# Image quarters on 128 partitions, folded normalisation, norms from the squared image and patches by chunk, in a patch-attention kernel

## The chip, the core and the metric

One NeuronCore of a Trainium2 chip. The time is that of one execution on the device, in microseconds (us). A core has TensorE (matmul, PE, with its weight loads PEld), VectorE (DVE), ScalarE (ACT), GpSimd (POOL), and SyncE (SP), which here issues DMAs.

## What is computed

The input x is 2 images of 32 channels, 48x48. Cut to what matters:

```python
x1 = x + L0(gn(x))            # gn: every channel of every image to mean 0, variance 1
out = x1 + dct2(gn(x1))       # cosine transform over rows and columns

# L0, per image:
embed = prelu(Wa x + ba)                            # 32 channels, 48x48
match = prelu(W1 x + b1)                            # 16 channels, 48x48
ref   = prelu(W2 mean2x2(x) + b2)                   # 16 channels, 24x24
w     = patches(ref, 3)                             # 576 keys of 144
w     = w / max(norm(w), 1e-4)
y     = softmax(10 * w @ patches(match, 3), axis=keys)     # 576 keys x 2304 queries
yt    = transposed_conv(y, patches(embed, 6, stride 2), stride 2)
return (conv(yt, Wd, 3x3, stride 2) + bd) / 6
```

All products are made nearly in fp32, from a high part (fp32r) and the low rest of each operand.

## The kernel before

**Queries.** The 2304 queries of an image are 6 groups of 384 (`CHUNK`): group t holds image rows t, t+6, t+12, ... Each group is 3 tiles of 128 queries, so there are 12 groups and 36 tiles for both images.

**Start (list `BEFORE`, image 0).** SyncE loads x three times, on partitions 0 to 95 (`load_x`), in a part of 768 columns and one of 1536. VectorE takes statistics (L893), GpSimd the power -1/2 (L444), VectorE normalises in two halves (L910), ScalarE rounds to fp32r (L733), VectorE makes the low part of the third copy (L918). A convolution is then one matmul per piece with high and low weights stacked over the 96 rows (L542 with four strided reads for the 2x2 mean, L549). ScalarE makes the negative and the positive part of each piece (L749, L751) and VectorE joins them with the slope into the padded images `wimg` and `mimg` (L942). SyncE's `im2col` copies 144 shifted rows to `wim`/`wim8` (keys) and `vim`/`v2` (queries), six transfers for each image, whole images at a time. The squares of the patches (L790, L791) give the norms by 12 fp32 matmuls (L579, L583), GpSimd the power -1/2 (L459), six matmuls spread it (L592), VectorE scales the keys (L995, L997) and the keys are split in high and low (L797, L798, L1004 to L1006). The embedding (L558, then L971, turned by L569 and split by L769 and L981) is made here too for image 0. The queries of groups 0 and 1 are split by ScalarE (L783, L785) and GpSimd (L468, L472); the first scores (L609) follow.

**Loop.** Step s makes on each engine, in a fixed order: scores of tile s+1 (TensorE, L609), their maximum (VectorE, L1010), the exponential with its sum (ScalarE, L807), its inverse (VectorE, L1017) and the normalisation (ScalarE, L815). GpSimd adds score tiles that meet in an output row (`row_sums`, L478). From step 9 on, three groups behind (`LAG`), the sums of group k are turned (`turn`, L629, five blocks), rounded and split (L823, L1025), multiplied with the embedding (`values`, L644), then with the 3x3 weights (`taps`, L656) and added into x1 (L1048). For t below 9 the scores use two buffers, later one.

**Between.** `SPREAD` puts the preparation of image 1 and the tail of image 0 at gaps: an entry (name, image, n, first, pace) puts part k at gap first + k*pace, that is at step (gap div 3), place (gap mod 3). Each engine performs its share at that place of its own stream, so that what stands behind waits too. `split` of group g stands at gap 9g-10. The buffer `pm` has two places that all small jobs take in turn (`misc`): part n waits until part n-2 has been emptied; `EMPTIES` says by which engine.

**SyncE's queue** is one stream in program order: for each image x, (image 0: parameters), x1's copy of x, (image 0: cosines, the nine blocks of output weights, L374), the patches of `wimg` (L359, L363), those of `mimg`. GpSimd splits the output weights (`output_weights`, L450, L451) between its parts of the start.

## Time and profile before

| | us |
|---|---|
| median of 3 runs (286.1 to 287.36) | 286.29 |
| the profiled execution | 286.1 |
| its span | 284.3 |
| TensorE busy | 216.6 (76%) |
| TensorE weight loads | 200.9 (71%) |
| VectorE busy | 154.6 (54%) |
| ScalarE busy | 137.5 (48%) |
| GpSimd busy | 94.5 (33%) |

The span reaches from the first to the last instruction; the rest of the 1.8 us lies around it. The profile's rows name the line, the engine, the operation, out<-in with the names of the tiles, their sizes and how often (x12). In a time line the first number is the start, the second the time that the group takes; what stands in brackets is how long the engine was idle before it and which work ended that. An fp32 matmul shows as two rows of the trace. "issue" means that nothing shown ended the wait. Granted clock 1.00 is the upper of TensorE's two levels where the throttle is concerned; how fast matmuls follow each other is read from their starts.

### The profile page before, as it was taken

What the parts mean: (1) busy time and instruction counts of PE and PEld (TensorE: products, weight loads), DVE (VectorE), ACT (ScalarE), POOL (GpSimd) and SP (SyncE); (2) the same over time, 40 slices, a digit from 0 to 9 for tenths busy, and PEclk for the clock granted to TensorE, in tenths of its full rate; (3) what the DMA queues carried; (4) which work ended last, traced back from release to release, by engine and by line L of the source; (5) the groups of instructions that cost most, each with busy time, mean ns of one, the idle gap of its engine ahead of it and who ended that gap; (6) DMA issues with size and microseconds to landing.
All of it is one profiled execution on the core that took longest, in us unless ns stands there. A gap on an engine that the chain in (4) does not pass through costs nothing.

```text
span 284.3 us, 4211 instructions
## 1 busy us (share of the span) xinstructions
PE 216.6 (76%) x1522; PEld 200.9 (71%) x1522; DVE 154.6 (54%) x303; ACT 137.5 (48%) x273; POOL 94.5 (33%) x96
## 2 busy tenths in 40 slices
PE   0064755653647998699998999999898999995085
...
## 3 DMA queue, kind: packets, MB, share of 16 engines
...
## 4 chain that ended last, share of the span: by engine, by line
PE 48%; DVE 20%; ACT 12%; issue 9%; SPq 5%; DMA 3%; POOL 2%; DVEq 0%; ACTq 0%; POOLq 0%
PE zt L629 22%; PE yt L644 8%; PE ps L609 6%; DVE negm L1010 4%; DVE bnst L893 4%; PE pm L676 3%; DVE yl L1025 3%; ACT nt L807 2%; SPq L363 2%; ACT zneg L749 2%; PE pd L656 2%; ACT z L751 2%; DVE v L1048 2%; DMA v<-mimg 2%; SPq L359 2%
## 5 line engine op out<-in xcount | busy, mean ns | idle before, releaser
L629 PE MATMUL zt<-ident,nt 128*125 128x128 f32 (+1 forms) x720 | 90.6, 277 | 0.0
L629 PEld LDWEIGHTS zt<-ident,nt 128*125 128x125 f32 (+1 forms) x720 | 87.4, 179 | 0.8
L478 POOL TENSOR_TENSOR nt<-nt 128x599 f32<-128x599 f32 (+1 forms) x42 | 56.9, 1354 | 32.2 <-ACT nt L815 25.0
L1025 DVE TENSOR_TENSOR yl<-zt,yh 125x384 fp32r<-125x384 f32 (+1 forms) x60 | 33.4, 557 | 46.2 <-ACT yh L823 18.2
L823 ACT ACTIVATE yh<-zt 125x384 fp32r<-125x384 f32 (+1 forms) x60 | 29.2, 486 | 36.9 <-PE zt L629 36.9
L807 ACT ACTIVATE nt<-ps,negm 128x576 f32<-128x576 f32 x32 | 23.8, 742 | 44.6 <-DVE negm L1010 44.6
L468 POOL TENSOR_TENSOR ml<-vim,mh 128x384 fp32r<-128x384 f32 x12 | 12.3, 1029 | 61.9 <-ACT mh L783 61.8
L815 ACT ACTIVATE nt<-nt,rps 128x599 f32<-128x599 f32 x36 | 28.7, 797 | 5.0 <-DVE rps L1017 4.8
L1048 DVE SCALAR_TENSOR_TENSOR v<-pd,v 32x384 f32<-32x384 f32 (+3 forms) x48 | 26.3, 547 | 2.6 <-PE pd L656 0.9
L1010 DVE TENSOR_REDUCE negm<-ps 128x1 f32<-128x576 f32 x32 | 24.1, 753 | 4.9 <-PE ps L609 4.7
L644 PE MATMUL yt<-yh,kh 125*128 125x384 f32 (+1 forms) x60 | 24.4, 407 | 2.5 <-DVE yl L1025 2.4
L609 PE MATMUL ps<-wh,mh 128*128 128x288 f32 x64 | 17.4, 357 | 11.6 <-ACT nt L807 6.2
L444 POOL TENSOR_TENSOR mv<-mv,mhalf 96x1 f32<-96x1 f32 (+1 forms) x4 | 2.2, 551 | 59.4 <-DVE mv L898 59.3
L609 PEld LDWEIGHTS ps<-wh,mh 128*128 128x128 f32 x64 | 11.4, 214 | 13.9 <-POOL mr L472 8.2
L644 PE MATMUL yt<-yh,kl 125*128 125x384 f32 (+1 forms) x60 | 20.4, 340 | 0.0
L644 PE MATMUL yt<-yl,kh 125*128 125x384 f32 (+1 forms) x60 | 20.4, 339 | 0.0
L542 PE MATMUL pm<-x,wst 96*96 96x288 f32 x16 | 5.2, 464 | 19.5 <-DVE x L918 19.5
L542 PEld LDWEIGHTS pm<-x,wst 96*96 96x96 f32 x16 | 3.6, 258 | 20.6 <-issue 15.5
L1017 DVE RECIPROCAL rps<-psm 128x1 f32<-128x1 f32 x36 | 5.9, 164 | 21.6 <-ACT nt L807 21.4
L609 PE MATMUL ps<-wl,mh 128*128 128x288 f32 x64 | 15.0, 320 | 0.0
L609 PE MATMUL ps<-wh,ml 128*128 128x288 f32 x64 | 14.7, 314 | 0.0
L609 PE MATMUL ps<-wr,mr 128*128 128x288 f32 x64 | 14.6, 313 | 0.0
...
## 6 DMA issues: line engine op xcount, KB each, us to landing
...
```

The lines of the kernel that those rows point to most:

```text
L468: link(pool.tensor_tensor(by_column_group(ml[:, k, :]), in_column_groups(vim[:, :], i), F(by_column_group(mh[:, k, :])), ALU.subtract))
L478: pool.tensor_tensor(nt[:, dst, (to + 1) * KP + 1:(to + 1) * KP + 1 + n], nt[:, one, (row1 + 1) * KP + 1:(row1 + 1) * KP + 1 + n], nt[:, o ...
L609: last = nc.tensor.matmul(scores_of(t)[:, i, 0:HALF], m[:, k, cols], w[b][:, HALF * i:HALF * (i + 1)], start=n == 0, stop=n == 3)
L629: last = nc.tensor.matmul(turned(zt[:, m % 2, :], n, dh, col, JW), keys_at(tile, r + dr, n, shift), ident[:, :], start=at == 0, stop=at == ...
L644: last = nc.tensor.matmul(yt[:, 0:CHUNK], e[b][0:n, blk, :], y[0:n, blk, :], start=blk == 0 and at == 0, stop=blk == KB - 1 and at == 2)
L807: nc.scalar.activation(strided(nt[:, tile_of(g, jb), :], KP + 1, (KP * HL // 2, 2), (KP, HL // 2), (1, WL)), strided(scores_of(t)[:, 0, :] ...
L815: nc.scalar.activation(tile, tile, ACT.Copy, scale=rps[:, k:k + 1]).then_inc(s_pn, 1)
L823: nc.scalar.activation(yh[0:n, blk, :].rearrange("p (h j) -> p h j", j=W), turned(zt[:, m % 2, :], n), ACT.Copy).then_inc(s_yh, 1)
L893: link(nc.vector.bn_stats(stats[rows, i, :], src[:, CHUNK * i:CHUNK * (i + 1)]))
L1010: nc.vector.tensor_reduce(negm[:, t % 2:t % 2 + 1], scores_of(t)[:, :, 0:HALF], AX.XY, ALU.max, negate=True).then_inc(s_mx, 1)
L1025: nc.vector.tensor_tensor(yl[0:n, blk, :].rearrange("p (h j) -> p h j", j=W), turned(zt[:, m % 2, :], n), F(yh[0:n, blk, :]).rearrange("p ...
L1048: nc.vector.scalar_tensor_tensor(out=image, in0=tap, scalar=1.0 / 6.0, in1=image, op0=ALU.mult, op1=ALU.add).then_inc(s_fin, 1)
```

## The change

- x comes in quarters: 576 columns of each channel on partitions 32q to 32q+31 (`x4`), for both images with buffers of their own. Statistics per quarter (2 x 288 columns) are averaged over the quarters by one matmul (`mean`), and the mean is subtracted and the scale applied not to x but to the weights (`weights`: nine operations on VectorE per image) and to the biases (`bias`: six fp32 matmuls and three operations). GpSimd adds 2x2 pixels (`pooled`).
- A convolution of a piece is three matmuls over 32 rows (high x high, high x low, low x high); conv2 and the embedding go in two quarters each, the embedding with 24 matmuls of 144 columns for each of two parts. The match convolution has eight pieces of 288 columns in place of six of 384.
- In every second piece VectorE makes the negative part itself; VectorE's last operation frees `pm`. 
- `mimg` holds the rows in the order of the groups, with a copied block before and behind, so a row of 48 is written once or twice more in 14 places. The match patches are copied by group: 36 transfers of 384 columns for each image, and `split` of a group waits for its own six.
- The norms come from the squared reference image: squares of three 32-row bands (two on ScalarE, one on GpSimd), 18 fp32 matmuls.
- Image 0's embedding moves into steps 1 to 4; the work of image 1 stands later. The parameters are loaded from ScalarE's queue; the output weights, the cosines and x1's copy come behind the match patches on SyncE's.

Cut to its core:

```diff
@@ tables
-EMPTIES = {"conv2": "act", "conv1": "act", "emb": "act", "ek": "dve", "norm": "dve", "inorm": "dve", "zn": "act", "d1": "dve",
+EMPTIES = {"mean": "dve", "bias": "dve", "conv2": "dve", "conv1": "dve", "emb": "dve", "ek": "dve", "norm": "dve", "inorm": "dve", "zn": "act", "d1": "dve",
 BEFORE = [
-    ("rows", (0, 1, 2)), ("scale", (0, 1)), ("low", (0, 1)), ("conv2", (0, 1)), ("conv1", (0, 1, 2, 3, 4, 5)),
-    ("squares", (0,)), ("norm", (0,)), ("inorm", (0, 1)), ("emb", (0, 1)), ("ek", (0, 1)), ("keys", (0,)), ("split", (0, 1))]
+    ("xs", (0,)), ("mean", (0,)), ("low", (0,)), ("weights", (0,)), ("bias", (0,)), ("conv2", (0, 1)),
+    ("conv1", (0, 1)), ("squares", (0,)), ("conv1", (2, 3, 4)), ("norm", (0,)), ("conv1", (5, 6, 7)),
+    ("inorm", (0, 1)), ("keys", (0,)), ("split", (0, 1))]
 SPREAD = [
-    ("residual", 0, 1, 4, 1), ("rows", 1, 3, 7, 1.5), ("scale", 1, 2, 12, 1), ("low", 1, 2, 13, 1),
-    ("conv2", 1, 2, 16, 1), ("conv1", 1, NCH, 19, 1), ("squares", 1, 1, 28, 1), ("norm", 1, 1, 30, 1),
-    ("inorm", 1, 2, 33, 1), ("keys", 1, 1, 37, 1), ("emb", 1, 2, 39, 1), ("ek", 1, 2, 41, 2), ("residual", 1, 1, 60, 1),
+    ("emb", 0, 2, 4, 2), ("ek", 0, 2, 9, 2), ("xs", 1, 1, 13, 1), ("mean", 1, 1, 15, 1), ("low", 1, 1, 17, 1),
+    ("weights", 1, 1, 20, 1), ("bias", 1, 1, 23, 1), ("residual", 0, 1, 28, 1), ("conv2", 1, 2, 26, 1),
+    ("conv1", 1, 8, 29, 1), ("squares", 1, 1, 33, 1), ("norm", 1, 1, 35, 1), ("inorm", 1, 2, 38, 1),
+    ("keys", 1, 1, 41, 1), ("emb", 1, 2, 46, 2), ("ek", 1, 2, 51, 2), ("residual", 1, 1, 60, 1),
@@ sync
+            def match_patches(b):
+                sp.wait_ge(s_const, 6)
+                sp.wait_ge(s_mimg[b], 1)
+                for t in range(NCH):
+                    if b:
+                        sp.wait_ge(s_split, NCH * (b - 1) + t + 1)
+                    im2col(mimg, 1 + CHUNK * t, CHUNK, CHUNK, vim, v2, slice(CHUNK * t, CHUNK * (t + 1)), s_mim[t])
...
+            load_x(0)
+            ref_patches(0)
+            match_patches(0)
+            sp.dma_start(x1(0), x[0].rearrange("c h w -> c (h w)")).then_inc(s_xin[0], 16)
+            load_x(1)
+            output_weights()
+            sp.dma_start(cosm[:, :], dct).then_inc(s_cos, 16)
+            sp.dma_start(x1(1), x[1].rearrange("c h w -> c (h w)")).then_inc(s_xin[1], 16)
+            ref_patches(1)
+            match_patches(1)
@@ gpsimd
-            first = before.index(("scale", 0, 1))
+            first = before.index(("low", 0, 0))
             perform(before[:first], handlers)
-            output_weights()
+            zeros()
+            pool.wait_ge(s_tiles, NTILE_EDGES)
             perform(before[first:], handlers)
+            output_weights()
             for s in range(steps):
@@ tensor
+            def conv(o, q, at, width, xh, xl):
+                rows = slice(C * q, C * (q + 1))
+                for n, (w, v) in enumerate(((wsh, xh), (wsh, xl), (wsl, xh))):
+                    last = nc.tensor.matmul(o, w[rows, at:at + width], v, start=n == 0, stop=n == 2)
+                return last
...
             def embed(b, i):
...
-                for n in range(4):
-                    last = nc.tensor.matmul(o[:, 0:HALF], wz[:, C * (3 - n):C * (7 - n)],
-                                            x3v[:, HL // 2 * i:HL // 2 * (i + 1), n // 2, :, n % 2],
-                                            start=n == 0, stop=n == 3)
+                for k in range(2):
+                    q = 2 * i + k
+                    rows = slice(C * q, C * (q + 1))
+                    if k:
+                        other_rows(last)
+                    dst = o[:, REFQ * k:REFQ * (k + 1)]
+                    parts = [v[rows, :].rearrange("p (i u j v) -> p i u j v", u=2, j=WL, v=2) for v in (x4h, x4l)]
+                    for n in range(4):
+                        at = S_WA + C * (3 - n)
+                        for m, (w, v) in enumerate(((wsh, 0), (wsh, 1), (wsl, 0))):
+                            last = nc.tensor.matmul(dst, w[rows, at:at + 128], parts[v][:, :, n // 2, :, n % 2],
+                                                    start=n + m == 0, stop=n == 3 and m == 2)
@@ scalar
+                if k % 2:
+                    nc.scalar.activation(zneg[0:rows, 1, :], o[0:rows, 0:HALF], ACT.Relu,
+                                         bias=nbias[0:rows, which:which + 1], scale=-1.0)
@@ vector, prelu
+                if k % 2:
+                    slope = nslope[0:rows, which:which + 1]
+                else:
+                    link(nc.vector.tensor_scalar(zneg[0:rows, 0, :], o[0:rows, 0:HALF], bias[0:rows, which:which + 1], 0.0,
+                                                 ALU.add, ALU.min))
+                for to, part in more:
+                    link(nc.vector.scalar_tensor_tensor(out=to, in0=part(zneg[0:rows, k % 2, :]), scalar=slope,
+                                                        in1=part(z[0:rows, k % 2, :]), op0=ALU.mult, op1=ALU.add))
```

How the streams move, at two places. GpSimd, from the last memset of the start to the first row sums, before (nt, wr and mr are tiles that are cleared, wdh and wdl the output weights' halves, ml and mr the queries' low parts):

```order
L440 MEMSET nt 128x30x24
L444 TENSOR_TENSOR mv<-mv,mhalf 96x1
L450 CAST wdh<-wdf 128x128
L451 TENSOR_TENSOR wdl<-wdf,wdh 128x128
L459 TENSOR_TENSOR nrm<-nrm,mhalf 96x6
L468 TENSOR_TENSOR ml<-vim,mh 128x8x3x16
L472 TENSOR_TENSOR mr<-v,mr 16x8x3x16
```

and with the change, from the norms on:

```order
L509 TENSOR_TENSOR nrm<-nrm,mhalf 96x6
L518 TENSOR_TENSOR ml<-vim,mh 128x8x3x16
L522 TENSOR_TENSOR mr<-v,mr 16x8x3x16
L518 TENSOR_TENSOR ml<-vim,mh 128x8x3x16
L522 TENSOR_TENSOR mr<-v,mr 16x8x3x16
L504 CAST wdh<-wdf 128x128
L505 TENSOR_TENSOR wdl<-wdf,wdh 128x128
L518 TENSOR_TENSOR ml<-vim,mh 128x8x3x16
L522 TENSOR_TENSOR mr<-v,mr 16x8x3x16
L528 TENSOR_TENSOR nt<-nt 128x624 x2
L475 TENSOR_TENSOR pairs<-x_1 128x288
L478 TENSOR_TENSOR x<-pairs 128x144
```

The output weights, before ahead of everything that patches feed, now stand behind two query splits and ahead of the third one, of the row sums and of image 1's pooling. VectorE, in steps 9 and 10 with the change (yl is the turned sums' low half, negm a maximum, rps an inverse sum):

```order
L1072 TENSOR_SCALAR zneg<-pm,bias 96x288
L1075 SCALAR_TENSOR_TENSOR mimg<-zneg,par,z 96x48
L1078 SCALAR_TENSOR_TENSOR mimg<-zneg,par,z 96x6x48
L1171 TENSOR_TENSOR yl<-zt,yh 125x384
L1156 TENSOR_REDUCE negm<-ps 128x1
L1075 SCALAR_TENSOR_TENSOR mimg<-zneg,nslope,z 96x48 x2
L1078 SCALAR_TENSOR_TENSOR mimg<-zneg,nslope,z 96x6x48
L1163 RECIPROCAL rps<-psm 128x1
```

and before, the same two steps:

```order
L1017 RECIPROCAL rps<-psm 128x1
L1025 TENSOR_TENSOR yl<-zt,yh 125x384 x2
L1010 TENSOR_REDUCE negm<-ps 128x1
L989 TENSOR_SCALAR nrm<-pm 96x6
L1017 RECIPROCAL rps<-psm 128x1
L1025 TENSOR_TENSOR yl<-zt,yh 125x384 x2
```

Image 1's match image is now written among the turned sums and maxima of these steps; before it was done by then.

## Rows read from the trace of the kernel before

**Rows 1.** Windows: stretch, its us, busy PE, PEld, DVE, ACT, POOL, PEclk, DMA share, GB/s.

```profile
61.20:87.30 26.10, 13.16 (x46) 10.62 (x46) 14.84 (x27) 17.49 (x36) 10.86 (x9) 0.57 0.10 16
87.30:107.00 19.70, 19.66 (x145) 19.50 (x146) 9.24 (x23) 12.78 (x27) 14.11 (x12) 0.88 0.00 1
107.00:131.30 24.30, 20.66 (x139) 19.75 (x137) 16.26 (x31) 14.65 (x32) 9.51 (x9) 0.93 0.59 67
131.30:261.60 130.30, 125.14 (x1001) 119.83 (x999) 76.56 (x147) 62.29 (x127) 43.23 (x36) 1.00 0.03 6
```

**Rows 2.** Time line of the start: start us, us, engine, line, operation [idle before <-releaser].

```profile
16.92 0.49 ACT L751 ACTIVATE z<-pm,par 96x288 f32<-96x288 f32 x1
...
19.55 0.08 DVE L949 MEMSET wimg<- 32x24 f32 x1
...
42.95 0.52 ACT L783 ACTIVATE mh<-vim 128x384 fp32r<-128x384 f32 x1 [0.57 <-DMA v<-mimg]
...
46.11 0.85 PE L609 MATMUL ps<-wh,mh 128*128 128x288 f32 x2 [5.44 <-POOL mr L472]
```

**Rows 3.** The same time line, DMA issues of SyncE's queue.

```profile
5.83 4.14 SPq L374 DMA_DIRECT2D wdf<-params  x9
...
19.72 1.95 SPq L359 DMA_DIRECT2D wim<-wimg  x3
...
25.55 4.92 SPq L359 DMA_DIRECT2D vim<-mimg  x3
```

**Rows 4.** DMA issues: kind, count, KB each, median us to landing.

```profile
wdf<-params SPq DMA_DIRECT2D x9, 4.0 KB, 2.4
```

**Rows 5.** Prices: groups of VectorE (mean ns), then TensorE in the time lines.

```profile
L942 DVE SCALAR_TENSOR_TENSOR wimg<-zneg,nslope,z 96x288 f32<-96x288 f32 x4 | 2.1, 516 | 3.6 <-ACT z L751 3.6
...
L1085 DVE TENSOR_TENSOR cosl<-cosm,cosh 96x96 fp32r<-96x96 f32 x1 | 0.3, 253 | 0.0
...
26.67 2.08 PE L579 MATMUL pm<-ones,sq 128*96 128x1 f32 x12 [3.49 <-ACT wim L791]
...
93.72 1.10 PE L579 MATMUL pm<-ones,sq 128*96 128x1 f32 x12
...
107.67 0.42 PE L609 MATMUL ps<-wh,ml 128*128 128x288 f32 x2
...
108.20 2.25 PE L558 MATMUL pm<-x,wz 96*128 96x288 f32 x8
```

**Rows 6.** Time line of the loop, steps 0 to 9.

```profile
51.15 0.74 ACT L807 ACTIVATE nt<-zt,negm 128x576 f32<-128x576 f32 x1
...
52.92 0.72 ACT L807 ACTIVATE nt<-ps,negm 128x576 f32<-128x576 f32 x1
...
59.09 1.00 POOL L468 TENSOR_TENSOR ml<-vim,mh 128x384 fp32r<-128x384 f32 x1 [10.88 <-ACT mh L783]
...
70.38 0.75 ACT L807 ACTIVATE nt<-ps,negm 128x576 f32<-128x576 f32 x1 [1.81 <-DVE negm L1010]
...
87.34 0.82 PE L609 MATMUL ps<-wh,mh 128*128 128x288 f32 x2 [2.35 <-ACT nt L807]
```

**Rows 7.** The same, VectorE operations beside GpSimd sums and without.

```profile
82.09 0.61 DVE L942 SCALAR_TENSOR_TENSOR mimg<-zneg,nslope,z 96x384 f32<-96x384 f32 x1 [1.83 <-ACT z L751]
...
83.88 1.24 POOL L478 TENSOR_TENSOR nt<-nt 128x599 f32<-128x599 f32 x1 [4.82 <-ACT nt L815]
...
84.77 0.77 DVE L942 SCALAR_TENSOR_TENSOR mimg<-zneg,nslope,z 96x384 f32<-96x384 f32 x1 [1.13 <-ACT z L751]
...
109.19 1.25 POOL L478 TENSOR_TENSOR nt<-nt 128x599 f32<-128x599 f32 x1 [1.46 <-ACT nt L815]
...
109.25 1.79 DVE L1005 TENSOR_TENSOR wr<-wim,wr 32x576 fp32r<-32x576 f32 x1
```

**Rows 8.** The same, TensorE behind the embedding of image 1.

```profile
116.10 1.22 PE L569 MATMUL pm<-ident,emb 128*125 128x128 f32 x4 [3.62 <-DVE emb L971]
```

459 lines of the change are left out of this document (269 added, 190 removed).

## The prediction

> **What bounds the kernel now.** I read the stretches first [rows 1], then the time line of the start [rows 2], the DMA issues of SyncE's queue and their time to landing [rows 3, 4], the prices of single operations [rows 5], the time line of the loop [rows 6, 7, 8]. The program has three parts. (1) Up to 46.1 us TensorE waits for the first scores: images, patches and keys of image 0. (2) Up to 87.3 us the softmax steps 0 to 8 run with no transposes yet; TensorE is busy for half of the time (13.2 of 26.1 us, at a granted clock of 0.57, much of it at the lower level) and the hand-over from maximum to exponential to normalisation, with image 1's preparation queued in between on ScalarE and VectorE, sets the pace. (3) From 87.3 to 261.6 us TensorE is the bound: 19.66 of 19.7, 20.66 of 24.3 and 125.1 of 130.3 us [rows 1]. A microsecond of TensorE work put there is a microsecond of time; one taken out of part 1 or 2 is worth it only if the chain of that part gets shorter. The tail is not touched. The profiled execution took 286.1 us, 1.8 more than its span; the median of the runs is 286.29, so a sum made on 286.1 stands for it.
>
> **Part 1, up to the first scores.** Before, the reference image was done at 19.6, the match image (its patches are issued at 25.55 [rows 3]), its patches had landed at 42.9 and scores began at 46.1 [rows 2]: the patches are the long piece (17.4 us), because their six transfers move whole images.
>
> *To the reference image.* Removed from VectorE's chain: six statistics of 384 columns become two of 288, two passes of normalisation and two low-half subtractions over 1152 columns go, the latter becomes one of 576 and one of 144. Added: the averaging matmul, four small VectorE operations, nine scalings and splits of weights, three of biases. The smallest VectorE operations take 0.15 to 0.25 us, as the 96x96 subtraction shows [rows 5], so these 16 cost about 3. The start's matmuls ran at about half of the later pace (12 norm passes in 2.08 and in 1.10 us [rows 5]), so I price them there as at the lower clock. The bias matmuls stand ahead of conv2 on TensorE: six in fp32 are twelve passes, 2.0 us. With x landed at 4.5 (four issues of 0.45 from 0.7 on and 2.0 to 2.4 to land [rows 4]), my estimates stage by stage: statistics 5.8, mean 6.9, root 7.6, splits of x 8.1, scaled weights 9.3, bias sums 11.4, first conv2 sums 13.1, both pieces through ScalarE and VectorE 16.4. Gain 3.2.
>
> *To the match image.* Six pieces of 384 columns become eight of 288. VectorE now makes the negative part of every even piece (0.45, under the 0.52 of an operation with one input more), writes the image (0.52) and 14 rows of 48 columns again for the neighbouring blocks. No such operation is in the trace; between 0.15 and the 0.25 of 96 columns I take 0.2 [rows 5]. That is 4 x 0.45 + 8 x 0.52 + 14 x 0.2 = 8.8 us of VectorE, and each piece's sums are freed only by its last operation, so TensorE (three matmuls, 0.8 us at the lower clock), ScalarE and VectorE take turns: about 1.5 us a piece, 12 for eight. Between piece 4 and 5 stand the norm sums: 18 rows, 36 passes, 6 us at the lower clock, 3.3 at the higher (1.10 us for 12) [rows 5]; about 1 of it is covered by piece 4. Match image at 16.4 + 12 + 5 = 33.4, eight later than before.
>
> *Patches and first scores.* Only the first chunk is waited for. Its six transfers are issued like those of the reference patches, 1.95 us for three [rows 3]: 4.0 with the waits between them, and 2.0 to land, under the 2.4 of rows 4 as they are few, at 39.5. ScalarE's and GpSimd's split took 3.2 us before (42.95 to 46.11) [rows 2]. The keys are ready by then: behind the match image come the norms' broadcast, four scalings of 288 columns, two roundings and three splits of up to 576, under 6 by the rates of rows 5. Scores start at about 42.7: **3.4 us earlier**.
>
> **Part 2: GpSimd is held.** GpSimd's stream takes in the output weights ahead of its part of the loop. Their nine small transfers now stand on SyncE's queue behind all 36 patch transfers, the residual x and image 1's quarters: 33.4 + 36 x 0.67 + 5 x 0.45 + 4.1 (the nine, [rows 3]) + 2.4 to land [rows 4] = 66.3. Rounding and splitting them is 1.5 us, to 67.8. What queues behind on GpSimd: the query split of group 2 (two operations of 1.0 [rows 6]), two sums of 1.3 to 1.4, and image 1's pooling (1.2 by its columns), so 73.8. ScalarE has the pooled x queued ahead of its normalisation 5: exponential 6 comes at about 75.0, 70.4 before [rows 6]. Before, it took 17.0 from there to the scores that open part 3 at 87.3 [rows 6], with image 1's convolutions in the way. Now mean, low halves, weights and biases are in the way (5.4 us of VectorE) but only one conv2 piece: three steps at 2.0 (unburdened ones are 1.8 apart, 51.15 to 52.92 [rows 6]), 11.4 in all. Part 3 opens at 86.4: **0.9 earlier**. Image 0's embedding, moved into steps 1 to 4 (48 matmuls of 144 columns, 7 us of TensorE), I cost at nothing: the hold covers it. If the hold went, it would pace steps 1 to 4.
>
> **Part 3: more work for the bound engine.** In 87.3 to 131.3, at the higher clock: norm sums 2.3 to 3.3 us; image 1's match convolution, before in part 2, 24 matmuls of 288 columns at 0.13 (0.42 for two that overlap, the next starting 0.27 after) 3.1; half of conv2 0.8; the embedding, 8 matmuls in 2.25, becomes 48 of half the columns at 0.14, 6.8. Sum +9.4. It can fill the 3.6 us that TensorE waited for the embedding's prelu [rows 8], since its jobs now stand five places apart. Against that, steps 9 to 12 get crowded. VectorE had 9.2 of 19.7 us there [rows 1]; with 8.8 of match image and 1.5 more it has 19.5. ScalarE's 12.8 becomes 22 with the pieces (12 x 0.49 [rows 2]), residual (2.2) and squares; TensorE has 24.6. Three nearly full engines that free each other's buffers don't run at the fullest one's pace; I put 2.4 there, between 0 and 6. **Net +8.2.** From 131.3 on nothing changes.
>
> Sum: 286.1 - 0.9 + 8.2 = 293.4, so 293.
>
> **A rule against the change.** VectorE's 384-column image write took 0.61 us with GpSimd idle, and 0.77 when a GpSimd sum ran until 0.35 after its start; the 576-column subtraction took 1.79 beside one that ended 1.19 after its start [rows 7]. So they ended 0.42 and 0.60 after the sum had, about what their columns take, as if they had waited for it.
> The Trainium skill ("SBUF — State Buffer", SBUF: two separate sides) says that a VectorE operation with two SBUF inputs and a GpSimd one that reads SBUF take a shared port pair as an exclusive lock; by that rule, the trace agrees.
> Steps 9 to 12 get 22 such writes where there were none, beside a GpSimd busy for 14.1 of 19.7 us [rows 1]. If each waits 0.7 (share) x 0.6 (half a sum), VectorE gets 9 us more; that it is on the path for half of it is rival B.
>
> **Rivals.** *B, VectorE becomes the bound of steps 9 to 12* through those waits: +5, 298. For: the row of 1.79. Against: the waits overlap TensorE's own.
> *C, GpSimd isn't held (faster).* If patch transfers are issued at the 0.46 of the output weights (nine in 4.14), 36 of them end 7.6 sooner; with the norm sums at the higher clock the whole queue starts 2.7 sooner. The output weights then come at 56, part 3 opens at 86.4 - 10.3 = 76.1, 11.2 earlier than before, and the sum is 286.1 - 11.2 + 8.2 = 283.1. It decides once the weights are in before 58. Against: the small patch transfers of rows 3 took 0.65 each.
> *D, the extra TensorE work finds room:* no crowding, the 3.6 filled, and the 2.3 us that the start of part 3 lost at the lower clock (granted clock 0.88 [rows 1]) come back: +9.4 - 5.9 - 0.9 = +2.6; with a norm at the higher clock in part 1 (-1.5) 287.2, no change.
> *E, the start doesn't get shorter:* pieces of 2 us and the whole norm in the way put the match image at 38.5 and everything on SyncE's queue 5 later: 298. The change would then not do what it says.
>
> **How the numbers follow.** Forecast 0.45, B 0.15, E 0.10, D 0.14, C 0.16. A measurement of this kernel tells 0.5% (1.4 us) from no change. Slower by more: forecast, B and E, 0.70; same: D, 0.14; faster: C, 0.16. The range leaves out most of C and the worst of B and E: 284.5 to 300.
>
> **What would show it.** Reference image near 16.4, match image near 33, first scores near 43; wdh on GpSimd near 66 right behind a DMA; exponential 6 near 75; part 3 opening near 86; TensorE's busy time in the loop 9 us up plus the embedding of image 0. Wrong, if GpSimd's weights come before 60, or if the stretch from the tenth step's scores to image 1's first scores (44.0 us before) grows by under 3.

## The result and the profile after

The changed kernel takes **324.82 us** (median of 4 runs, 323.96 to 326.36); the kernel before took 286.62 on the same chip (4 runs). The ratio is 1.1336, 95% interval 1.1282 to 1.1391: 38 us slower. The forecast was 293, with a range up to 300. The sign was right, the size was short by 31 us. The profiled execution has a span of 324.6 us, 40.3 more than before; it is the longest of the four, and the profiled one of before (286.1) is the shortest of its four. A few executions are over 1.5% slower than the fastest of their kernel; ratios and intervals leave these out, while a time is the median of all.

First the stretches between the same events as in [rows 1]: first scores, the tenth step's scores, image 1's first scores (columns as there).

```profile
0.00:46.40 46.40, 21.14 (x98) 17.88 (x98) 25.88 (x71) 12.61 (x24) 13.08 (x27) 1.00 0.18 33
46.40:92.70 46.30, 32.07 (x153) 29.30 (x154) 19.53 (x47) 20.33 (x42) 16.62 (x17) 0.72 0.23 46
92.70:169.50 76.80, 69.57 (x357) 63.34 (x358) 41.24 (x84) 34.41 (x69) 26.86 (x22) 0.68 0.16 27
169.50:302.00 132.50, 125.99 (x1006) 120.46 (x1004) 77.25 (x149) 62.98 (x129) 41.54 (x35) 1.00 0.03 6
```

Against before: start 46.4 (46.1), steps 0 to 8 46.3 (41.2), from there to image 1's first scores 76.8 (44.0), all that follows 155.1 (153.0). So +0.3, +5.1, +32.8 and +2.1. The third stretch holds four fifths of the loss, and TensorE's granted clock in it is 0.68, where it was 0.88 and 0.93 [rows 1]. As one stretch, before:

```profile
87.30:131.30 44.00, 40.31 (x282) 39.26 (x282) 25.50 (x53) 27.43 (x58) 23.62 (x20) 0.91 0.33 38
```

Of the 32.8 us, 29.3 are busy time of TensorE (69.6 for 40.3) and only 3.5 are time in which it is idle (7.2 for 3.7). I count each matmul record up to the start of the next one, or to its own end if that is sooner. Then the old work (transposes, scores, products with the embedding, 3x3 weights) takes 46.9 us where it took 33.9, +13.1, with the same 232 records. Image 1's preparation takes 22.7 where it took 6.5, +16.2: 7.7 for conv2 and conv1, 7.8 for the embedding (2.1 before), 5.8 for the norm sums (2.1 before). The last 2.1 us of the loss lie directly behind image 1's first scores, where the embedding's turning now stands (L670, and 1.0 us of waiting behind it).

The start, in its time line:

```profile
5.50 0.68 ACT L830 ACTIVATE x4h<-x 128x576 fp32r<-128x576 f32 x1 [2.08 <-DMA x<-x]
...
9.88 0.74 POOL L462 MEMSET mr<- 128x768 f32 x1
...
12.60 2.15 DVE L1047 CAST wsh<-wsf 128x96 fp32r<-128x96 f32 x2
...
19.22 0.08 DVE L1086 MEMSET wimg<- 32x24 f32 x1
...
26.17 5.89 PE L681 MATMUL pm<-ones,sq 96*96 96x1 f32 x36 [0.22 <-DVE mimg L1078]
...
38.63 1.86 SPq L373 DMA_DIRECT2D vim<-mimg  x3
...
43.68 0.52 ACT L871 ACTIVATE mh<-vim 128x384 fp32r<-128x384 f32 x1 [1.50 <-DMA v<-mimg]
...
46.45 0.85 PE L707 MATMUL ps<-wh,mh 128*128 128x288 f32 x2 [6.61 <-POOL mr L522]
```

The reference image is ready at 19.3 as before, the patches of the match image are issued at 38.6. Two roundings of 96 columns took 2.15 us while GpSimd was clearing tiles; the same two for image 1, at 85.96 with GpSimd idle, took 0.43. The norm sums alone are 5.89 us.

Steps 0 to 8, GpSimd and what follows from it:

```profile
64.64 4.14 SPq L405 DMA_DIRECT2D wdf<-params  x9
...
70.08 0.29 POOL L504 CAST wdh<-wdf 128x128 fp32r<-128x128 f32 x1 [19.12 <-DMA wdf<-params]
...
72.97 0.85 PE L707 MATMUL ps<-wh,mh 128*128 128x288 f32 x2 [5.67 <-POOL mr L522]
...
77.01 0.32 ACT L832 ACTIVATE x2h<-x 128x144 fp32r<-128x144 f32 x1 [5.30 <-POOL x L478]
77.92 0.73 ACT L899 ACTIVATE nt<-ps,negm 128x576 f32<-128x576 f32 x1
...
92.72 0.58 PE L707 MATMUL ps<-wh,mh 128*128 128x288 f32 x1 [0.39 <-ACT nt L899]
```

GpSimd stands still for 19.1 us in front of the output weights. TensorE waits 5.67 for the query split behind them, and ScalarE 5.30 for the pooled x. Exponential 6 starts at 77.92 (70.38 before [rows 6]).

The third stretch by groups (line, engine, operation, count, busy us, mean ns, idle before and its releaser):

```profile
L727 PE MATMUL zt<-ident,nt 128*125 128x128 f32 (+1 forms) x125 | 25.2, 373 | 0.0
...
L742 PE MATMUL yt<-yh,kh 125*128 125x384 f32 (+1 forms) x12 | 6.3, 527 | 1.1 <-DVE yl L1171 1.1
...
L681 PE MATMUL pm<-ones,sq 96*96 96x1 f32 x36 | 5.9, 298 | 0.4 <-DVE mimg L1078 0.4
...
L660 PE MATMUL pm<-x4h,wsh 32*128 32x144 f32 x16 | 5.4, 335 | 0.1
...
L1078 DVE SCALAR_TENSOR_TENSOR mimg<-zneg,par,z 96x288 f32<-96x288 f32 x4 | 4.5, 1126 | 0.1
...
L621 PE MATMUL pm<-x4h,wsh 32*96 32x288 f32 x8 | 3.7, 459 | 4.7 <-DVE mimg L1078 4.7
```

The records of an engine overlap, so the rows can't be summed, but their means can be compared: the turning transposes take 373 ns each here, and 294 in the same stretch before:

```profile
L629 PE MATMUL zt<-ident,nt 128*125 128x128 f32 (+1 forms) x126 | 17.8, 294 | 0.0
```

So the old work runs slower. Of the new work some does and some doesn't:

```profile
122.80:128.70 5.90, 5.90 (x37) 5.90 (x38) 2.03 (x5) 1.12 (x3) 0.00 (x0) 0.50 0.00 0
151.90:155.30 3.40, 3.34 (x24) 3.03 (x23) 1.19 (x3) 1.59 (x4) 3.17 (x4) 0.98 0.46 77
162.10:163.50 1.40, 1.40 (x9) 1.27 (x7) 0.00 (x0) 0.00 (x0) 0.00 (x0) 0.50 0.04 12
```

The first is the norm sums, wholly at the lower level. The second is most of the embedding's first half: its matmuls start 0.13 us apart, at the upper level. The last six of its second half (in the third line) start 0.21 apart, at the lower. Of the eight pieces of the match convolution, four take 0.5 us and four (from 105.58, 109.72, 121.36 and 131.71 on) 0.8. And TensorE waits 4.7 us in front of conv pieces for VectorE's writing of the image. The time line of the longest of these waits shows what the write stood beside:

```profile
102.41 2.81 POOL L528 TENSOR_TENSOR nt<-nt 128x624 f32<-128x624 f32 x2 [2.82 <-ACT nt L907]
...
103.80 1.73 DVE L1078 SCALAR_TENSOR_TENSOR mimg<-zneg,par,z 96x288 f32<-96x288 f32 x1
...
105.58 0.55 PE L621 MATMUL pm<-x4h,wsh 32*96 32x288 f32 x1 [2.61 <-DVE mimg L1078]
...
109.14 0.52 DVE L1078 SCALAR_TENSOR_TENSOR mimg<-zneg,nslope,z 96x288 f32<-96x288 f32 x1
```

The write takes 0.52 alone. It takes 1.73 when it starts as the second of two row sums of GpSimd (1.4 each) does, and ends 0.3 after that sum. The Trainium skill ("SBUF — State Buffer", SBUF: two separate sides) has such a pair take turns for a whole instruction; by that rule, the trace agrees.

### The profile page after: what moved, and what is told of

It is laid out like the page before. It is cut to its first block, busy times and chain, and to the rows that moved or that the text cites. A ratio compares the mean times of both kernels' runs of the same rounds, so it can differ in the third digit from the quotient of the medians.

```text
span 324.6 us, 4740 instructions
## 1 busy us (share of the span) xinstructions
PE 259.4 (80%) x1698; PEld 240.2 (74%) x1698; DVE 173.8 (54%) x368; ACT 133.1 (41%) x269; POOL 98.6 (30%) x101
## 4 chain that ended last, share of the span: by engine, by line
PE 51%; DVE 20%; issue 9%; SPq 9%; ACT 6%; POOL 2%; DMA 2%; DVEq 0%; ACTq 0%; POOLq 0%
PE zt L727 20%; PE yt L742 8%; PE ps L707 5%; PE pm L681 4%; SPq L377 3%; SPq L373 3%; PE pm L621 3%; DVE negm L1156 3%; PE pm L774 3%; PE pm L660 2%; DVE mimg L1078 2%; DVE yl L1171 2%; DVE bnst L988 2%; PE pd L754 2%; DVE mimg L1075 2%
## 5 line engine op out<-in xcount | busy, mean ns | idle before, releaser
L727 PE MATMUL zt<-ident,nt 128*125 128x128 f32 (+1 forms) x720 | 98.0, 290 | 0.0
L727 PEld LDWEIGHTS zt<-ident,nt 128*125 128x125 f32 (+1 forms) x720 | 94.0, 191 | 1.4 <-issue 0.3
L1171 DVE TENSOR_TENSOR yl<-zt,yh 125x384 fp32r<-125x384 f32 (+1 forms) x60 | 33.4, 557 | 43.9 <-ACT yh L915 15.2
L707 PE MATMUL ps<-wh,mh 128*128 128x288 f32 x64 | 18.3, 372 | 17.0 <-POOL mr L522 12.3
L1156 DVE TENSOR_REDUCE negm<-ps 128x1 f32<-128x576 f32 x32 | 24.1, 753 | 13.1 <-PE ps L707 13.0
L742 PE MATMUL yt<-yh,kh 125*128 125x384 f32 (+1 forms) x60 | 25.6, 427 | 4.6 <-DVE yl L1171 4.5
L518 POOL TENSOR_TENSOR ml<-vim,mh 128x384 fp32r<-128x384 f32 x12 | 12.1, 1005 | 49.4 <-ACT mh L871 49.2
L707 PEld LDWEIGHTS ps<-wh,mh 128*128 128x128 f32 x64 | 11.6, 222 | 19.5 <-POOL mr L522 12.7
L742 PE MATMUL yt<-yh,kl 125*128 125x384 f32 (+1 forms) x60 | 21.5, 359 | 0.0
L742 PE MATMUL yt<-yl,kh 125*128 125x384 f32 (+1 forms) x60 | 21.3, 356 | 0.0
L851 ACT ACTIVATE z<-pm,bias 96x288 f32<-96x288 f32 (+1 forms) x24 | 11.7, 491 | 16.2 <-PE pm L621 12.1
L484 POOL TENSOR_TENSOR mv<-mv,mhalf 32x1 f32<-32x1 f32 x2 | 1.1, 544 | 56.4 <-DVE mv L993 56.4
L742 PEld LDWEIGHTS yt<-yh,kh 125*128 125x128 f32 (+1 forms) x60 | 12.1, 201 | 7.5 <-DVE yl L1171 6.7
L621 PE MATMUL pm<-x4h,wsh 32*96 32x288 f32 x16 | 7.8, 496 | 10.3 <-DVE mimg L1078 9.1
```

The costliest lines, as they stand in the source:

```text
L621: last = nc.tensor.matmul(o, w[rows, at:at + width], v, start=n == 0, stop=n == 2)
L707: last = nc.tensor.matmul(scores_of(t)[:, i, 0:HALF], m[:, k, cols], w[b][:, HALF * i:HALF * (i + 1)], start=n == 0, stop=n == 3)
L727: last = nc.tensor.matmul(turned(zt[:, m % 2, :], n, dh, col, JW), keys_at(tile, r + dr, n, shift), ident[:, :], start=at == 0, stop=at == ...
L742: last = nc.tensor.matmul(yt[:, 0:CHUNK], e[b][0:n, blk, :], y[0:n, blk, :], start=blk == 0 and at == 0, stop=blk == KB - 1 and at == 2)
L1156: nc.vector.tensor_reduce(negm[:, t % 2:t % 2 + 1], scores_of(t)[:, :, 0:HALF], AX.XY, ALU.max, negate=True).then_inc(s_mx, 1)
L1171: nc.vector.tensor_tensor(yl[0:n, blk, :].rearrange("p (h j) -> p h j", j=W), turned(zt[:, m % 2, :], n), F(yh[0:n, blk, :]).rearrange("p ...
```

## The experiments

Two theories run through them. The first, A or A' in the earlier expectations and S in the later ones: the changed work itself (more TensorE pieces, 32-row operands, copied rows) costs the time. The second, B in the earlier ones (not the prediction's rival B) and P in the later: its place does, since it now stands in full steps. For most runs the exponentials' starts were also read from the time lines. This table has how many us later than before they came; a column that grows to the next names the stretch where the time went (exponential 10 came at 90.94 before, 35, the last, at 211.53). Each row is one profiled execution, so that differences of a us or two in it aren't firm.

| kernel | 0 | 3 | 6 | 10 | 13 | 17 | 19 | 35 |
|---|---|---|---|---|---|---|---|---|
| changed | 0.3 | 1.4 | 7.5 | 5.8 | 27.0 | 30.9 | 40.3 | 40.2 |
| all rows | 0.7 | 1.8 | 7.9 | 6.1 | 25.8 | 27.6 | 33.4 | 33.4 |
| norm third | 0.9 | 3.3 | 7.5 | 5.7 | 22.7 | 27.1 | 36.8 | 36.8 |
| no copied rows | 0.4 | 2.9 | 7.6 | 5.8 | 19.3 | 21.1 | 30.8 | 30.8 |
| one product | 0.4 | 1.4 | 7.4 | 5.6 | 25.8 | 24.8 | 29.1 | 29.0 |
| image 1 early | 0.3 | 1.3 | 9.8 | 24.6 | 26.1 | 32.9 | 33.0 | 32.9 |
| embedding 0 first | 12.7 | 10.6 | 7.7 | 5.9 | 25.9 | 27.3 | 36.7 | 36.6 |
| before, image 1 late | 0.0 | -2.2 | -7.3 | -10.9 | -4.5 | -0.8 | 3.7 | 4.7 |
| before, chunks | -3.1 | -4.2 | -1.1 | 1.9 | 7.1 | 8.1 | 8.1 | 8.5 |
| before, chunks, embedding first | 2.0 | -0.1 | -0.1 | 3.0 | 8.3 | 8.3 | 8.3 | 8.4 |
| all small | 0.7 | 1.7 | 0.6 | -1.6 | 8.1 | 7.0 | 10.5 | 10.4 |
| all small, early | 0.7 | 2.4 | 8.4 | 14.5 | 15.8 | 12.1 | 12.1 | 12.0 |
| all small, ScalarE frees | -2.8 | -2.1 | -3.1 | -6.1 | 3.0 | 3.7 | 7.2 | 7.1 |

### One cost taken out at a time

**All rows.** Image sums are then taken over all four quarters, so the numbers differ; the sizes of the matmuls in columns are the same. The edit stands in all four places where rows are chosen, for both images.

```diff
-                rows = slice(C * q, C * (q + 1))
+                rows = slice(0, 128)
```

> The convolutions' and the embedding's matmuls read all 128 rows of x and of the weights in place of the 32 of one quarter, so their sums are those of four quarters (wrong values, same columns, same number of matmuls, same order). Measured with the change: 324.8 us, the stretch from the tenth step's scores to image 1's first scores 76.8 us at a granted clock of 0.68, against 44.0 us at 0.91 before. Theory A (TensorE is kept at the lower level because it works with a quarter of its rows): the clock of that stretch rises above 0.85 and the time falls by 10 us or more, to 305 to 315. Theory B (it falls because VectorE and GpSimd make it wait): 323 to 327, clock within 0.05. Theory C (the one-column norm passes): 323 to 327 too.

Measured 319.46, ratio 1.1143 (1.1062 to 1.1224), 5.4 less. The result lies between the windows of the theories. The clock did rise: over the whole kernel it was 0.892 to 0.895 in the three executions, and 0.848 to 0.854 in the four of the changed kernel. The third stretch is now:

```profile
93.04:162.70 69.66, 56.89 (x358) 53.51 (x359) 40.73 (x84) 34.30 (x69) 26.41 (x21) 0.83 0.18 30
```

With as many and as wide matmuls, TensorE is busy for 12.7 us less (56.9 for 69.6), at a granted clock of 0.83 in place of 0.68, and the turning transposes take 313 ns in place of 373. But the stretch is only 7.1 us shorter, since TensorE's idle time grew from 7.2 to 12.8: it now waits 8.4 us for the image's writes, where it waited 4.7. The other engines stand close behind it.

A single window tells little of the clock, since what falls into it shifts from run to run. Here is 130 to 140 us in the changed kernel, in this one and in *norm third*, whose convolutions have 32 rows:

```profile
130.00:140.00 10.00, 10.00 (x50) 9.39 (x49) 4.12 (x11) 3.76 (x8) 4.93 (x5) 0.59 0.15 25
```

```profile
130.00:140.00 10.00, 10.00 (x69) 10.00 (x68) 6.58 (x17) 5.30 (x12) 3.80 (x4) 0.83 0.16 28
130.00:140.00 10.00, 10.00 (x69) 10.00 (x68) 6.84 (x17) 5.01 (x10) 1.95 (x2) 0.83 0.32 54
```

The Trainium skill ("TensorE: Matmul & The Clock Gate", Part 1) says that activity releases the throttle. The profile's busy time alone doesn't show this here: it is 10.00 of 10 us at 0.59 and at 0.83. What the run shows is that over the whole kernel 32-row operands, in the place of 128-row ones, go with a lower clock. It can't separate the rows from what switching between 32-row and 128-row operands may cost in itself.

**Norm third.** Image 1's norm sums over one of three rows.

```diff
-                    for r in range(3):
+                    for r in range(1 if b else 3):
...
-                                                stop=r == 2)
+                                                stop=r == (0 if b else 2))
```

> Image 1's norm sums are cut to 6 of 18 rows (12 of 36 passes), so two of three patch rows are missing from its norms. Theory C: the 36 passes of one column take 5.9 us and keep the lower clock as well; then 3.9 us come off directly and the work around them speeds up, 8 us or more in all, to 317 or less. Theories A and B: 3 to 4 us at most, 321 to 322.

Measured 323.43, ratio 1.1283 (1.1193 to 1.1373): 1.4 less, which the intervals don't tell from nothing; it fits none of the windows. In the table, exponentials 10 to 35 lose 31.1 where they lost 34.4. Theory C, that the norm passes hold the clock down, gets nothing from it: 0.845 to 0.850 over the kernel, as in the changed one.

**Weights early.** The output weights' nine transfers right behind x on SyncE's queue.

```diff
             load_x(0)
+            output_weights()
             ref_patches(0)
```

> The nine blocks of output weights are issued right behind image 0's quarters, ahead of its patches, so that GpSimd has them 45 us sooner. My part 2 (GpSimd is held by them until 70 us and holds the query split of group 2): scores 6 come some 5 us sooner and the time falls by 3 to 6 us, to 319 to 322. Rival: ScalarE's own queue is as late (image 1's x is still issued behind the patches), then under 1.5 us.

Measured 319.26, ratio 1.1102 (1.0948 to 1.1256), 5.6 less: the hold of GpSimd is worth about what was expected. The interval rests on two executions (316.38 and 319.26) and is wide, 2 to 11 us.

**No copied rows.** Image 1's 14 operations of 48 columns left out (the blocks' borders are then wrong).

```diff
-                above = [first] * (i > 0)
-                below = [last] * (i < ROWS - 1)
+                above = [first] * (i > 0 and not b)
+                below = [last] * (i < ROWS - 1 and not b)
```

> Image 1's 14 copied rows of 48 columns are not written (its patches then hold image 0's rows there). They took 0.27 us each and up to 1.5 beside GpSimd. Rival B of my prediction (VectorE, held up by GpSimd's sums, paces steps 9 to 12): 8 us or more off, to 316 or less. If VectorE isn't the pace: 2 to 4 us off.

Measured 319.37, ratio 1.1104 (1.0989 to 1.122), 5.4 less. The 14 operations are 5.2 us of VectorE by the changed kernel's profile (7 of 426 and 7 of 320 ns, 0.27 each when alone; alone they would be 3.8). The loss is about their whole length, but the interval, some 3 to 10 us, can't tell it from the other readings, and the result lies between the two windows. In the table most of it comes between exponentials 10 and 13.

**One product.** High x high alone in image 1's conv2, conv1 and embedding.

```diff
-            def conv(o, q, at, width, xh, xl):
+            def conv(o, q, at, width, xh, xl, one=False):
...
-                for n, (w, v) in enumerate(((wsh, xh), (wsh, xl), (wsl, xh))):
-                    last = nc.tensor.matmul(o, w[rows, at:at + width], v, start=n == 0, stop=n == 2)
+                pairs = ((wsh, xh),) if one else ((wsh, xh), (wsh, xl), (wsl, xh))
+                for n, (w, v) in enumerate(pairs):
+                    last = nc.tensor.matmul(o, w[rows, at:at + width], v, start=n == 0, stop=n == len(pairs) - 1)
...
-                        for m, (w, v) in enumerate(((wsh, 0), (wsh, 1), (wsl, 0))):
+                        pairs = ((wsh, 0),) if b else ((wsh, 0), (wsh, 1), (wsl, 0))
+                        for m, (w, v) in enumerate(pairs):
```

The calls of `conv` for image 1 pass `b == 1` as `one`.

> The changed kernel with one of three products (high x high alone) in image 1's conv2, conv1 and embedding: 20, 24 and 48 matmuls less two thirds each. If TensorE's time for these pieces sets the pace, two thirds of 16.1 us (conv 8.1, embedding 8.0) fall out: 312 to 316 us. If VectorE, which empties the accumulators, sets it, TensorE only waits longer: 320 us or more.

Measured 315.48, ratio 1.0997 (1.096 to 1.1033), 9.3 less, in the window for TensorE's time; it is the largest single part. That it nearly is the 10.7 that two thirds would be is a coincidence of two things, as the table shows. Up to exponential 13, where conv2 and conv1 stand, only 1.2 us are gained. Behind it, up to exponential 19, 10.0 are. The changed kernel's stretch, then this one's:

```profile
132.61:177.32 44.71, 41.67 (x254) 39.65 (x254) 23.00 (x48) 20.25 (x43) 15.04 (x12) 0.82 0.22 37
```

```profile
131.41:166.15 34.74, 31.31 (x221) 29.28 (x220) 22.74 (x48) 20.02 (x43) 15.02 (x12) 0.95 0.28 48
```

TensorE's time for the embedding falls from 7.8 to 2.9, which is half of the 10.0. The other half is the old work beside it, which runs faster (granted clock 0.95 for 0.82). So the convolution's matmuls counted for little in their own steps, and the embedding's for about twice their length.

### Its place

**Image 1 early.** The changed kernel with image 1's load and work at about before's places (weights 12, conv1 17, norm 26, embedding 39), the output weights early too.

```diff
-    ("weights", 1, 1, 20, 1), ("bias", 1, 1, 23, 1), ("residual", 0, 1, 28, 1), ("conv2", 1, 2, 26, 1),
-    ("conv1", 1, 8, 29, 1), ("squares", 1, 1, 33, 1), ("norm", 1, 1, 35, 1), ("inorm", 1, 2, 38, 1),
+    ("weights", 1, 1, 12, 1), ("bias", 1, 1, 13, 1), ("conv2", 1, 2, 15, 1), ("conv1", 1, 8, 17, 1),
+    ("squares", 1, 1, 24, 1), ("norm", 1, 1, 26, 1), ("residual", 0, 1, 28, 1), ("inorm", 1, 2, 30, 1),
...
-    ("keys", 1, 1, 41, 1), ("emb", 1, 2, 46, 2), ("ek", 1, 2, 51, 2), ("residual", 1, 1, 60, 1),
+    ("keys", 1, 1, 34, 1), ("emb", 1, 2, 39, 2), ("ek", 1, 2, 43, 2), ("residual", 1, 1, 60, 1),
```

> The change with weights and image 1's quarters issued ahead of the patches, and image 1's preparation 6 to 12 gaps earlier (convolution at gaps 17 to 24, squares 24, norm 26, keys 34, embedding 39 and 41). By now all rows in the convolutions gave 5 us and a third of the norm passes 2 us, so most of the 38 us is open. Theory B (crowding where TensorE is the bound): 300 to 310. Theory A' (the work itself, wherever it stands): 312 to 318, that is 1 to 7 under the kernel with the weights early (319.3).

Measured 320.17, ratio 1.1131 (1.1033 to 1.1228). The weights alone had given this; both windows were missed, that of A' by 2. The table shows 24.6 us lost by exponential 10 in place of 5.8, and 8.3 behind it in place of 34.4: moved as a whole, the changed work costs the same at both places. The theory that the loss comes from its place falls.

**Before, image 1 late.** The other way round: the kernel before with its own image 1 work (and image 0's residual) at the changed kernel's places.

```diff
-    ("residual", 0, 1, 4, 1), ("rows", 1, 3, 7, 1.5), ("scale", 1, 2, 12, 1), ("low", 1, 2, 13, 1),
-    ("conv2", 1, 2, 16, 1), ("conv1", 1, NCH, 19, 1), ("squares", 1, 1, 28, 1), ("norm", 1, 1, 30, 1),
+    ("residual", 0, 1, 28, 1), ("rows", 1, 3, 11, 1.5), ("scale", 1, 2, 16, 1), ("low", 1, 2, 17, 1),
+    ("conv2", 1, 2, 26, 1), ("conv1", 1, NCH, 29, 1), ("squares", 1, 1, 35, 1), ("norm", 1, 1, 36, 1),
...
-    ("inorm", 1, 2, 33, 1), ("keys", 1, 1, 37, 1), ("emb", 1, 2, 39, 1), ("ek", 1, 2, 41, 2), ("residual", 1, 1, 60, 1),
+    ("inorm", 1, 2, 38, 1), ("keys", 1, 1, 41, 1), ("emb", 1, 2, 46, 2), ("ek", 1, 2, 51, 2), ("residual", 1, 1, 60, 1),
```

> The kernel before with nothing but the places of image 1's preparation changed to nearly those of the change (convolution at gaps 29 to 34, squares 35, norm 36, keys 41, embedding 46 and 48; residual at 28). Theory B (place): it loses 8 to 20 us, to 295 to 306, with the clock of steps 9 to 14 falling to 0.7. Theory A' (the changed work): steps 0 to 8 get shorter by what leaves them and steps 9 to 16 longer by the 6 us of TensorE work: 283 to 290.

Measured 289.97 (9 runs), ratio 1.0129 (1.0096 to 1.0162), 2.9 more: inside the window of A', at its end. It hides two large terms: 10.9 us gained by exponential 10, 15.6 lost behind it. This is the most instructive row of the table: it prices the old work in the crowded steps, 15.6 us, where I had put 3.9 for the matmuls of the moved pieces and 2.4 for crowding. The changed kernel pays 34.4 there, so the changed form of the work is 19 us dearer, and it doesn't get the 10.9. What differs is shown by the stretch from exponential 10 to 19, before, here, and in the changed kernel:

```profile
90.94:137.05 46.11, 42.47 (x310) 41.22 (x310) 27.92 (x55) 28.39 (x61) 28.22 (x23) 0.95 0.32 37
```

```profile
80.06:140.72 60.66, 48.73 (x318) 45.92 (x317) 33.64 (x68) 36.81 (x75) 28.34 (x24) 0.89 0.28 35
```

```profile
96.69:177.32 80.63, 72.46 (x394) 66.58 (x394) 43.35 (x89) 36.36 (x74) 27.91 (x23) 0.72 0.15 26
```

The old work at the late places costs 6.3 us of busy time and 8.3 of idle time of TensorE, and the clock stays near before's, not at the 0.7 that theory B expected. The changed work costs 30.0 of busy time and 4.5 of idle time. So the place brings waits, and the lower clock comes with the changed work.

**Embedding 0 first.** The changed kernel with image 0's embedding ahead of the first scores.

```diff
-    ("inorm", (0, 1)), ("keys", (0,)), ("split", (0, 1))]
+    ("inorm", (0, 1)), ("emb", (0, 1)), ("ek", (0, 1)), ("keys", (0,)), ("split", (0, 1))]
```

> The changed kernel with image 0's embedding and its turning back ahead of the first scores, where the kernel before has them. Exponential 6 came 7.5 us later than before, and most of that appeared in the steps of the embedding. If the embedding in the loop costs that (at the lower clock, between small steps), the start grows by 3 to 5 us and the sixth exponential is no later than now; the end is 318 to 324 us. If the loss up to exponential 6 is the late output weights on GpSimd alone, the start's growth comes on top: 326 to 330 us.

Measured 325.57, ratio 1.1359 (1.131 to 1.1407): no difference, between the two windows. Its time line:

```profile
61.88 0.76 ACT L899 ACTIVATE nt<-ps,negm 128x576 f32<-128x576 f32 x1 [5.08 <-DVE negm L1156]
...
70.18 0.29 POOL L504 CAST wdh<-wdf 128x128 fp32r<-128x128 f32 x1 [9.58 <-DMA wdf<-params]
...
73.09 0.85 PE L707 MATMUL ps<-wh,mh 128*128 128x288 f32 x2 [3.53 <-POOL mr L522]
```

The first exponential comes 12.7 us later and the sixth at the same time, behind the same output weights at 70. Up to there 12 us that stand between the match image and the first scores cost nothing: the hold covers them, as the prediction said of the embedding. They don't delay SyncE's queue, so the output weights come when they did.

### The kernel before with parts of the change

**Before, chunks.** Eight pieces, match image and patches by groups, copied rows, image 0's embedding in the loop, image 1's x loaded before the patches, residual at 28; arithmetic, statistics and norms as before.

```diff
-                im2col(b, mimg, s_mimg[b], W, Q, vim, v2, s_mim[b])
+                ref_patches(b)
+                match_patches(b)
```

> The kernel before with the one part of the change that should pay: the match image in group order (eight pieces of 288 columns, 14 copied rows), its patches copied and waited for by group; image 0's embedding (in its old form of 8 matmuls) in steps 1 to 4; image 1's x loaded ahead of the patches; output weights where they were; image 1's preparation in its old places. First scores should come at 39 (46.1 before), set by the keys. If that carries through: 278 to 282, faster than both. If the copied rows and the embedding in steps 1 to 4 eat it: 284 to 288.

Measured 294.58, ratio 1.0239 (1.0139 to 1.0339). The start is 3.1 us shorter, and the end 8 later; both windows were missed. With the embedding ahead of the first scores:

```diff
-    ("emb", 0, 2, 4, 2), ("ek", 0, 2, 8, 2), ("residual", 0, 1, 28, 1), ("rows", 1, 3, 7, 1.5),
+    ("residual", 0, 1, 28, 1), ("rows", 1, 3, 7, 1.5),
```

> The kernel before with the match image written by chunks and its patches loaded by chunks (the earlier hybrid, 294.6 us), but image 0's embedding ahead of the first scores. The earlier hybrid started 3.1 us sooner and had lost 3.9 us by the eighth exponential, where the embedding lay. If the embedding in the loop was that loss: 288 to 291 us. If it was the chunked transfers running beside the loop: 293 to 296 us.

Measured 294.47, ratio 1.0275 (1.0239 to 1.0311). The first exponential is 5.1 later than in the last run, exponentials 3 to 7 are as before, and the end is the same. So my reading that the embedding was the loss fell, and the shorter start was never worth anything here, where the output weights come early: the steps up to exponential 6 absorb it. The result lies in the window for the chunked transfers, but doesn't show that they are the cause.

**Without its copied rows** (image 1's borders wrong, edit as above):

> The last hybrid (before's arithmetic, chunked match image, embedding first, 294.5 us) without image 1's 14 copied rows. It loses 8.4 us between exponentials 7 and 12. If VectorE's copied rows (14 of 0.27 us and more beside GpSimd) are that loss: 288 to 290 us. If it is the eight pieces or the moved residual: 293 us or more.

Measured 290.92, ratio 1.0127 (1.0081 to 1.0174), 3.6 less, just above the window for the copied rows. **The residual alone moved**, in the kernel before:

```diff
-    ("residual", 0, 1, 4, 1),
+    ("residual", 0, 1, 28, 1),
```

> The kernel before with one move alone: image 0's residual convolution from place 4 to place 28, where the changed kernel has it. If that piece is free in the early steps and costs its length in the full ones: 287.5 to 290 us. If it holds the early steps: 283 to 286 us.

Measured 289.39 (8 runs), ratio 1.0062 (1.0023 to 1.0102), 1.8 us. Its exponential 10 comes 1.8 us sooner and its last 3.1 later, so that this one piece may be 4.9 of the 15.6 us of *before, image 1 late*. Copied rows 3.6 and residual 1.8 are most of the hybrid's 7.6. **Image 1's embedding moved ahead**, in the kernel before:

```diff
-    ("emb", 1, 2, 39, 1), ("ek", 1, 2, 41, 2),
+    ("emb", 1, 2, 26, 1), ("ek", 1, 2, 40, 1),
```

> The kernel before with one move alone: image 1's embedding from place 39 to place 26, ahead of the steps in which TensorE is full. If TensorE's full steps make a piece dear, its 8 matmuls and their VectorE work come out of the path: 284 to 285.5 us. If the early steps are as full on VectorE: 286.5 to 289 us.

Measured 289.21 (12 runs), ratio 1.0082 (1.0054 to 1.011): slower by 0.8%, just outside the second window. No version tried beats the kernel before.

### All of it together

**All small**: all rows (for both images), one product, norm third and no copied rows for image 1, output weights early.

> The changed kernel with all suspected costs of image 1's preparation taken down together: its convolutions and embedding with one of three products and over all 128 rows, the norm sums over one of three rows, no copied rows, and the output weights loaded right after x. Theory S (the loss is the sum of these pieces of work): the single removals gave -5.4, -1.4, -5.4 and -5.6 us, and two thirds of the 16 us of TensorE time of convolution and embedding should give 6 to 10 more: 290 to 300 us. Theory P (the place of the work and its waits cost the time, whatever its size): at least 308 us.

Measured 297.04, ratio 1.037 (1.0319 to 1.0421): 27.8 us less. The five single removals gave 5.4 + 1.4 + 5.6 + 5.4 + 9.3 = 27.1. By the ratios, which leave the chips out, they gave 30 together, and 27.7 all at once. They add up within the noise, and 22 of the 38 us come off when image 1's changed work is made smaller, and nearly 6 with the output weights' place. **The same at the early places:**

> The combination of small work (297.0 us) with image 1's preparation also at the earlier places, where the steps wait for one another and TensorE is busy 4 of 10 us. With the full work these places gave nothing (320.2 against 324.8, while the weights alone gave 5.6). If place matters once the work is small, most of the last 10 us go: 287 to 292 us. If the size of the remaining work is all: 295 to 299 us.

Measured 297.68, ratio 1.0378 (1.034 to 1.0416): again place is worth nothing. A part of what is left shows in the waits of TensorE in *all small*, from 88 to 122 us (waited for, us, times, longest):

```profile
PE pm L622 <- DVE mimg L1080: 5.5, 4, 3.2
PE pm L683 <- DVE mimg L1080: 1.4, 1, 1.4
```

The old kernel gave an accumulator back behind ScalarE's second read, the changed one behind VectorE's image write. **ScalarE frees** undoes that, in the changed kernel and in *all small*:

```diff
-                if k % 2:
-                    nc.scalar.activation(zneg[0:rows, 1, :], o[0:rows, 0:HALF], ACT.Relu,
+                nc.scalar.activation(zneg[0:rows, k % 2, :], o[0:rows, 0:HALF], ACT.Relu,
...
-                                     bias=bias[0:rows, which:which + 1]).then_inc(s_z, 1)
+                                     bias=bias[0:rows, which:which + 1]).then_inc(s_free["act"], 1)
```

> The changed kernel with one change: ScalarE reads both signs' parts of every conv and embedding piece and gives the accumulator back, as in the kernel before; VectorE then only writes the image. If the accumulator's return behind VectorE's write is a cause, the 4.7 us for which TensorE waits in front of conv pieces go, and the late conv pieces no longer hold the score turns behind them: 314 to 320 us. If it is not: 322 us or more, ScalarE having more work.

> The same change in the combination of small work (297.0 us). TensorE waits 5.5 us there in front of conv pieces for VectorE's image write. If that is what is left of the loss: 289 to 293 us. If not: 295 us or more.

Measured 321.43, ratio 1.1181 (1.1102 to 1.1259), 3.4 less; and 293.23, ratio 1.0232 (1.0193 to 1.0271), 3.8 less. Both missed their windows by a little. The table has the gain ahead of exponential 10 (the first exponential comes 3.5 us sooner than in *all small*, exponential 10 comes 4.5 sooner), and behind it *all small* lost 12.0 and this one 13.2. In the loop the wait only changed its name:

```profile
PE pm L622 <- ACT z L852: 5.2, 3, 2.0
PE pm L683 <- ACT z L852: 2.0, 1, 2.0
```

So the accumulator's return was a cause in the start, and in the loop the edit gained nothing. In the changed kernel with this edit, the match image's patches are issued at 35.15 in place of 38.63, and the output weights come 3.9 sooner:

```profile
66.13 0.29 POOL L504 CAST wdh<-wdf 128x128 fp32r<-128x128 f32 x1 [18.96 <-DMA wdf<-params]
```

Its exponential 6 is 3.9 us sooner than in the changed kernel, and its end 3.4. So a match image that is ready sooner does pay there, through SyncE's queue. 6.5 us stay open: by *the residual alone* some 1.8 of it is the residual's place; the rest wasn't taken apart.

## Why the prediction was right or wrong

- **Part 1, first scores 3.4 us earlier: wrong**, 0.3 later. Of my stage times the first to miss is x (5.5 for 4.5), then the weights: the first conv2 matmul started at 14.99, where its sums were to be ready at 13.1, with VectorE's roundings beside GpSimd's memsets. The norm sums had been priced at 6 and took 5.89. From reference to match image it was 19.4 for 17.0, which makes 38.6 for 33.4. This is rival E's event, and its 38.5 is met to the number in part by luck: E had eight pieces of 2 us from 16.4 on, and they took 1.7 from 19.3 on. What stands behind the match image hardly matters: 12 us more there (*embedding 0 first*) and 5 more in the hybrid cost nothing. The match image itself matters, since the output weights are queued behind its patches: 3.5 us of it were worth 3.4 (*ScalarE frees*).
- **Part 2, 0.9 earlier: wrong in size, 5.4 later; GpSimd held: right in mechanism.** wdh at 70.1 for 66.3, most of the start's 5.2 carried into it; exponential 6 at 77.9 for 75.0; the hold was worth 5.6. From there to the opening 14.8 for 11.4: image 1's weights stand there on VectorE beside row sums (one of its operations took 1.34 us, where the same one took 0.26 in the start), a chain that I had at plain rates. Opening at 92.7 for 86.4. Image 0's embedding cost nothing, as said.
- **Part 3, +8.2: wrong, +32.8.** This is the step that failed, and in it the term **TensorE's work at +9.4 "at the higher clock"**. TensorE's busy time grew by 29.3: the new work by 16.2 for 9.4, and the old work by 13.1, for which the sum had nothing. The granted clock was 0.68 in the stretch, where before it was 0.91; the old transposes took 373 ns for 294. In the new work the norm sums (+3.6 for +1.0) ran at the lower level, and the convolutions (7.7 for 3.9) half of their pieces; the embedding was priced nearly right (+5.8 for +4.5) and ran mostly at the upper one. I took the clock of before for a property of the stretch; it is one of what runs there. The rows of the operands are a part of it (0.83 with 128 rows); what else keeps it from before's 0.91 stays open.
- **Crowding at 2.4, "between 0 and 6".** Together with the 3.6 that were to be filled, this term was to give -1.2. In the changed kernel TensorE's idle time grew by 3.5. So as waiting it was off by 4.7, far less than the first term. But the waits are larger where TensorE's work is smaller: they grew by 8.3 in *before, image 1 late*, and are 12.8 in *all rows* against the changed kernel's 7.2. The old work had been cheap in steps that wait anyway, and I had costed the move by its matmuls only (3.1 and 0.8), not by the ScalarE and VectorE work behind each piece. The bound "6" had no row behind it.
- **"From 131.3 on nothing changes": +2.1**, from the embedding's turning, which now stands behind image 1's first scores.
- **What the move should have given back.** *Before, image 1 late* was 10.9 us ahead at exponential 10. The changed kernel was 5.8 behind. The output weights are a part of this: with them early *all small* was 1.6 ahead there, while none of the other removals in it moved exponential 10 by more than 0.3. That the pooled x and the new weights are the rest is argued from the time line. I had seen the hold and missed what it hid.
- **Rivals.** B: held writes are in the trace (1.73 for 0.52) and TensorE waits for them, but freeing the accumulator elsewhere gained nothing in the loop; the copied rows' 5.4 is the part that a run shows. VectorE was busy for 41 of the 76.8 us, so it was not full. C and D had no part: the weights came late, and no room was found. E's event came true. Its price of 5 is borne out by *ScalarE frees*, where 3.5 us of start were worth 3.4, but it is a small part of the 38.
